# Second product of the self attention with the values stationary, turned back once for four heads

## The reference, cut to what matters

```
x = x + L0_xattn(ctx, ctx, layernorm(x))      # 16 heads of 16
h = layernorm(x)
q, k, v = h @ Wq.T + bq, h @ Wk.T + bk, h @ Wv.T + bv      # 16 heads of 16
scores = q @ k.T / 4                          # 256 x 256 for each head
top_scores, top_idx = top_k(scores, 64)
w = softmax(top_scores)
out = sum_k w[k] * v[top_idx[k]]
x = x + out @ Wo.T + bo
...
```

## Time and profile before

| | |
|---|---|
| median of 3 runs | 1896.39 us (1888.04 to 1904.47) |
| the profiled execution | 1896.86 us, span of its core 1895.4 us |
| TensorE busy | 1518.8 us, 80% of the span |
| VectorE busy | 1291.2 us, 68% |
| ScalarE busy | 984.9 us, 52% |
| GpSimd busy | 402.0 us, 21% |
| granted TensorE clock, mean | 0.896 |

### The profile page before, as it was taken

One profiled execution on the slowest core, in us unless ns is written; L12 is line 12 of the kernel. 1 busy time (PEld: TensorE's weight loads), 2 busy tenths in 40 slices (PEclk: granted clock), 3 DMA queues, 4 the chain that ended last, 5 costly groups with the idle time before them and its releaser, 6 DMA issues. The chain is left out here.

```text
span 1895.4 us, 30782 instructions
## 1 busy us (share of the span) xinstructions
PE 1518.8 (80%) x11554; PEld 910.3 (48%) x11554; DVE 1291.2 (68%) x3823; ACT 984.9 (52%) x1423; POOL 402.0 (21%) x258
## 2 busy tenths in 40 slices
PE   4999999998898988899598979999355666456579
PEld 2555566665555555555355747576212223122243
DVE  3000198887787878778889999512549995699845
ACT  2888777876667757667335434434153331543100
POOL 5000022222221222112211212100104440344200
PEclk9999999999989999989788989999677777687879
DMA  9433333321232213200502221430000000000010
GB/s 165 98 80 68 69 68 68 68 57 35 46 68 57 40 41 68 57 24 2 179 23 67 90 89 45 128 95 1 25 0 0 0 0 0 0 0 0 0 51 17
DMA packets 48209, 94.32 MB, mean 50 GB/s; under 512 B 13345, under 2 KB 36521, under 8 KB 44977
## 3 DMA queue, kind: packets, MB, share of 16 engines
q1 hardware_dynamic: 48048, 92.22, 20.6%
HBM read 91.15 MB, written 1.05 MB: 49 GB/s over the span
## 5 line engine op out<-in xcount | busy, mean ns | idle before, releaser
L982 ACT ACTIVATE attn_arena<-ps 128x1024 f32<-128x1024 f32 x512 | 496.0, 1023 | 224.7 <-PE ps L356 222.8
L356 PE MATMUL ps<-attn_arena 32*128 32x256 f32 x4096 | 377.5, 413 | 6.6 <-ACT attn_arena L982 4.4
L1330 DVE MATCH_REPLACE8 attn_work<-attn_top,attn_work 128x256 f32<-128x256 f32 x896 | 359.4, 408 | 0.0
L1327 DVE MAX8 attn_top<-attn_work 128x8 f32<-128x256 f32 x896 | 332.8, 413 | 0.0
L356 PEld LDWEIGHTS ps<-attn_arena 32*128 32x128 f32 x4096 | 254.7, 190 | 81.9 <-issue 43.3
L368 PE MATMUL ps<-attn_arena 128*32 128x256 f32 x4096 | 286.8, 397 | 5.5 <-issue 5.1
L900 POOL TENSOR_SCALAR attn_pm<-attn_work 128x512 f32<-128x512 f32 x64 | 95.7, 1495 | 643.4 <-DVE attn_work L1330 643.4
L1673 DVE TENSOR_TENSOR_SCAN ssm_h<-ssm_decay,ssm_bu 128x1024 f32<-128x1024 f32 x64 | 219.4, 3467 | 8.2 <-POOL ssm_bu L1466 4.8
L1466 POOL TENSOR_TENSOR ssm_bu<-ssm_brow,ssm_du 128x2048 f32<-128x2048 f32 x32 | 144.6, 4522 | 270.9 <-ACT ssm_brow L1512 230.1
L368 PEld LDWEIGHTS ps<-attn_arena 128*32 128x32 f32 x4096 | 109.9, 111 | 143.8 <-issue 85.1
L1582 PE MATMUL ps<-ssm_hc,ident 128*128 128x512 f32 x256 | 155.1, 763 | 4.5 <-DVE ssm_hc L1678 4.5
(11 more groups left out here) (251 smaller groups left out, 1867.1 us busy)
## 6 DMA issues: line engine op xcount, KB each, us to landing
attn_arena<-ctxT SPq DMA_DIRECT2D x64, 256.0 KB, 8.0
attn_arena<-ctxV SPq DMA_DIRECT2D x16, 1024.0 KB, 13.0
attn_arena<-maskT SPq DMA_DIRECT2D x32, 512.0 KB, 3.7
attn_arena<-ctxT SPq DMA_DIRECT2D x32, 512.0 KB, 4.9
attn_arena<-ctx SPq DMA_DIRECT2D x16, 1024.0 KB, 5.9
ffn_w<-w SPq DMA_DIRECT2D x2, 1024.0 KB, 6.7
X<-x SPq DMA_DIRECT2D x4, 256.0 KB, 3.3
out<-X SPq DMA_DIRECT2D x4, 256.0 KB, 2.2
```

The lines of the kernel that those rows point to most:

```text
L356: mm = pe.matmul(ps[:, first + j - 2 * i, u * S:(u + 1) * S], kx[n % 2][rows, k0:k0 + P], qpad[rows, n % GROUPS, b * S:(b + 1) * S], start ...
L982: act.activation(probs[m % 2][:, 2 * i:2 * i + 2], ps[:, first:first + 2, :], ACT.Exp, scale=1.0 / 16.0).then_inc(exp_done, 1)
L1327: dve.max(top[:, t, turn], s[:, i, t] if turn == 0 else work[:, i, t]).then_inc(picked, 1)
L1330: dve.match_replace(work[:, i, t], top[:, t, turn], s[:, i, t] if turn == 0 else work[:, i, t], LOW).then_inc(picked, 1)
```

## The change

`products` makes the values stationary (32 columns from the head's first, so the next head's columns come along and are not used) and the turned weights move, 256 columns. Head j of a group writes partitions 32j to 32j+31 of `M_`. It is two matmuls a head. `take_sums` copies those 32 partitions, 256 columns, to a new tile `accS`. When the four heads of a group are there, TensorE turns `accS` back with two transposes (`turn_sums`), in slot 0 of step p for the group that ends with head p-2, behind `turn_pm` of head p-1. `divide_self` reads the turned sums from PSUM, and it moves to the end of turn 1's jobs. The semaphore `ao_ready` is gone: `turn_ao` waits for the job's turn in `M_`. The tile v gets 15 more columns and loses its fourth dimension.

```
-        v = sb("v", [P, 2 * T, H, VP])
+        v = sb("v", [P, 2 * T, H * VP + 32 - VP])
+        vh = v[:, :, 0:H * VP].rearrange("p k (h d) -> p k h d", d=VP)
...
-        sums = sb("sums", [P, T, HG, VP])
+        accS = sb("accS", [P, S])
...
+                head = (g * HG + j) * VP
+                for k in range(T):
+                    mm = pe.matmul(M_[32 * j:32 * j + 32, 0:S], v[:, b % 2 * T + k, head:head + 32], pT[:, :, k, :], start=(k == 0), stop=(k == T - 1))
+                mm.then_inc(misc_made, 1)
+
+            def turn_sums(b, g):
+                pe.wait_ge(misc_taken, misc["sums", (b * GROUPS + g + 1) * HG - 1] + 1)
+                begin("self", b, g)
                 for t in range(T):
-                    for k in range(T):
-                        mm = pe.matmul(M_[:, t * VP:(t + 1) * VP], pT[:, t, k, :], v[:, b % 2 * T + k, g * HG + j, :], start=(k == 0), stop=(k == T - 1))
+                    mm = pe.transpose(M_[:, t * P:(t + 1) * P], accS[:, t * P:(t + 1) * P], ident[:])
                 mm.then_inc(misc_made, 1)
 
             def turn_ao(b):
-                pe.wait_ge(ao_ready, GROUPS * (b + 1))
+                pe.wait_ge(misc_taken, misc["self", b, GROUPS - 1] + 1)
...
                         if 0 <= done < B * H:
                             turn_pm(done)
+                        if 0 <= p - 2 < B * H and (p - 2) % HG == HG - 1:
+                            turn_sums(*where(p - 2)[0:2])
...
             def take_sums(p):
-                b, g, j = where(p)
-                if j == 0 and p:
-                    act.wait_ge(ao_ready, GROUPS * b + g)
-                take_misc(sums[:, :, j, :], M_[:, 0:T * VP].rearrange("p (t v) -> p t v", t=T), "sums", p)
+                rows = slice(32 * where(p)[2], 32 * where(p)[2] + 32)
+                take_misc(accS[rows, :], M_[rows, 0:S], "sums", p)
...
             def divide_self(p):
                 b, g, j = where(p)
-                dve.wait_ge(misc_taken, misc["sums", p] + 1)
-                step(dve.reciprocal(srecip[:], sums[:, :, :, D]))
...
+                dve.wait_ge(misc_made, misc["self", b, g] + 1)
+                turned = M_[:, 0:S].rearrange("p (t j v) -> p t j v", t=T, j=HG)
+                step(dve.reciprocal(srecip[:], turned[:, :, :, D]))
...
-                    if 0 <= p - 2 < B * H and (p - 2) % HG == HG - 1:
-                        divide_self(p - 2)
                     for b in due_after("out", p):
...
                     for b in due_after("octx", p):
                         add(b, "octx")
+                    if 0 <= p - 2 < B * H and (p - 2) % HG == HG - 1:
+                        divide_self(p - 2)
```

More of the change, by code:

```diff
@@ L314, in attention @@
         sel_ready, pm_ready, pm_turned, pT_ready = sem("sel_ready"), sem("pm_ready"), sem("pm_turned"), sem("pT_ready")
-        ao_ready = sem("ao_ready")
         moe_loaded, moe_consts, lmax_ready, den_ready = sem("moe_loaded"), sem("moe_consts"), sem("lmax_ready"), sem("den_ready")
@@ L1212, in add_v @@
                 dve.wait_ge(misc_made, misc["v", b] + 1)
-                dve.tensor_tensor(v[:, b % 2 * T:(b % 2 + 1) * T, :, 0:D], M_.rearrange("p (t h d) -> p t h d", t=T, d=D),
+                dve.tensor_tensor(vh[:, b % 2 * T:(b % 2 + 1) * T, :, 0:D], M_.rearrange("p (t h d) -> p t h d", t=T, d=D),
                                   bv[:].rearrange("p (h d) -> p h d", d=D).unsqueeze(1).to_broadcast([P, T, H, D]), ALU.add).then_inc(misc_taken, 1)
@@ L1217, in divide_self @@
                 b, g, j = where(p)
-                dve.wait_ge(misc_taken, misc["sums", p] + 1)
-                step(dve.reciprocal(srecip[:], sums[:, :, :, D]))
-                dve.tensor_tensor(ao[:, :, g * HG * D:(g + 1) * HG * D].rearrange("p t (j d) -> p t j d", d=D), sums[:, :, :, 0:D],
-                                  srecip[:].unsqueeze(3).to_broadcast([P, T, HG, D]), ALU.mult).then_inc(ao_ready, 1)
+                dve.wait_ge(misc_made, misc["self", b, g] + 1)
+                turned = M_[:, 0:S].rearrange("p (t j v) -> p t j v", t=T, j=HG)
+                step(dve.reciprocal(srecip[:], turned[:, :, :, D]))
+                dve.tensor_tensor(ao[:, :, g * HG * D:(g + 1) * HG * D].rearrange("p t (j d) -> p t j d", d=D), turned[:, :, :, 0:D],
+                                  srecip[:].unsqueeze(3).to_broadcast([P, T, HG, D]), ALU.mult).then_inc(misc_taken, 1)
             def choose(b):
```

## The result

The changed kernel takes 1900.08 us (median of 20 runs, 1891.46 to 1904.02), the kernel before 1893.11 us (20 runs, 1882.23 to 1904.47). The ratio is 1.0037, 95% interval 1.0022 to 1.0051: 7 us slower (4 to 10), where 16.4 us were forecast. The profiled execution took 1901.18 us, 1899.6 us from first to last instruction, against 1895.4 before, at a mean granted clock of 0.909 against 0.896.

A forecast was written before the change was run, and what follows sets the result against it. TensorE and ScalarE were taken to set the early pace, VectorE the late one, through GpSimd. Terms: 3.4 (product, turning, copy) + 12.5 (wait) + 0.5 (tail) = +16.4 us on 1896.9, so 1913 us; range 1893 to 1930.

The forecast's parts named there:

- The product on TensorE: Each head's second self attention product: 0.15 us saved by one shape change less, -6.6 us for 44 heads beside L368.
- Turning back: Two new transposes behind turn_pm in slot 0: 0.3 us in each of 11 steps, +3.3 us, plus 0.5 behind head 63.
- The copy: ScalarE's copy of the sums grows from 194 to about 378 ns; the next M_ job waits 37 times: +6.7 us.
- The wait on VectorE: The division at turn 1 waits for transposes behind turn_pm: about 42 us in 15 groups, +12.5 us reaching the end.
- cover in the early steps: In eight steps from 5 to 41, TensorE's waits for ScalarE's exponentials hide VectorE's delay; together 0.5 us remains.
- step 13: A batch's cross attention ends here; the division comes 2.9 us later, only 0.27 is free, so about 2.5 us counts.
- step 61: TensorE waits for GpSimd here, so VectorE's later division counts in full: +1.9 us.
- rival 4: The clock: TensorE idles longer before its pm turns, and two or three more half-clock stretches cost 8 to 11 us; chance 0.10.
- step 46: Follows step 45, where a batch's cross attention ends and the late division was to add about 2.5 us without cover.
- two signs against itself: Wrong if heads 4 to 12's period leaves 54.2 by over 1 us, or L1219 waits yet the last head ends at most 5 us later.

The follow-up runs named there:

- half product: The changed kernel with 128 instead of 256 moving columns in the product and a copy of 34 columns: 1887.38 us, ratio 0.9965 to the kernel before.
- old form with 119 columns: The kernel before, each matmul of its second product moving 119 instead of 17 columns, of which 17 are copied: 1891.68 us, ratio 0.9994.
- short copy: The changed kernel with ScalarE copying 34 instead of 256 columns of each head's 32 partitions: 1894.24 us, ratio 1.0012 to the kernel before.
- short product: The changed kernel with the product moving 17 instead of 256 columns and ScalarE copying those 17: 1874.22 us, ratio 0.9901 to the kernel before.
- the wait alone: The kernel before, with VectorE's division also waiting for the pm transposes of the next step's slot 0: 1907.59 us, ratio 1.0077.
- four heads at once: The changed kernel with turn_sums first and one product and copy per four-head group: 1844.49 us; with the division in turn 3 as well, 1820.13 us.

## Why the prediction was wrong

**The product on TensorE** was right in length: 0.15 us a head forecast, 0.11 + 0.04 read. That all 44 savings lie on the path was not tested in this form, and the half product shows that in some steps a shorter product brings nothing. **Turning back** was right in kind (273 ns a transpose, in slot 0). **The copy** was near: 362 ns for the 378 assumed, 4.7 us measured for 6.7.

**The wait on VectorE** was right in size: 46.3 us of waiting for 42, cover in the early steps, 2.7 for 2.5 us in step 13, 1.9 for 1.9 in step 61; 14 to 15 us for 12.5 when it is added or taken away alone. TensorE's waits for GpSimd grew as said, from 234 to 1208 us; the group of L482 before, and then after:

```profile
L482 PE MATMUL ps<-ident,attn_pm 128*128 128x128 f32 x256 | 44.3, 299 | 42.0 <-POOL attn_pm L903 42.0
```
```profile
L482 PE MATMUL ps<-ident,attn_pm 128*128 128x128 f32 x256 | 45.2, 303 | 53.8 <-POOL attn_pm L912 53.8
```

With the measured wait and copy the terms make -6.6 + 3.3 + 0.5 + 4.7 + 14.6 = +16.5 us, and 7.0 (4 to 10) was measured. Some 9 us are missing; the copy and the wait carry intervals of 5 to 6 us to either side, so this figure is no sharper than that.

**The step that failed is the clock**, which the sum held constant and rival 4 let only fall, because TensorE would stand idle longer in front of its pm turns. It did stand idle longer, and the mean clock rose from 0.898 to 0.907. I had looked at the product's length alone, not at what it moves in that time: before, eight matmuls of 17 columns; after, four of 256, in the same 1 us.

What 0.01 of clock is worth, in us:
- the old form with 119 columns: 3.7 us of work added, -1.1 seen, 4.8 won (0 to 10) for 0.0049: 10
- among the runs of one kernel each, the time falls by 16 to 18 (before, three sets of 23 to 29 runs) and 13 (after, 20 runs); this goes with the clock, and by itself does not say which of the two is the cause
- short copy to half product: 18.8 us of work taken away, 8.9 seen, so at most 9.9 lost for 0.0087: 11
- short copy to short product: 33.1 taken away, 21.0 seen, at most 12.1 lost for 0.0103: 12.

The last two are upper ends, since they count all the work taken away as work on the path. At 10 to 18 us the rise of 0.0091 would bring 9 to 16 us; that much is an estimate.

**A second thing was overlooked: step 46.** The forecast has 2.5 us for heads 44 to 46, without cover, and the trace has -4.0, because TensorE's idle time ahead of L435 fell from 9.54 to 4.51 us. This is not the clock and not one execution's luck. The stretch takes 34.3 to 35.1 us, with 8.9 to 9.5 us ahead of L435, in the four profiles of the old form without the wait, and 28.7 to 31.4 us, with 2.9 to 5.9, in all eight of the new form, those with a mean clock as low as before included. With the wait alone it is 33.5 and 6.5 us. What TensorE waits for there, and why the new form shortens it, stays open.

The clock and step 46 together give back more than is missing, if both are taken at their full size. How the 9 us divide between them is not shown. Two rows speak for a small part of the clock: after head 46 it rose most (0.92 for 0.87 from 917 us on), and the time there is longer by just the 5.7 us forecast; and up to head 44 only 1.6 us of the forecast are missing. The profiled pair also began its head 0 2.5 us apart, which no term explains.

The prediction had named two signs against itself, and neither came: the period of heads 4 to 12 changed by 0.4 us, and the last head does end over 5 us later. Counted from the start of head 0, VectorE starts head 63 6.1 us later than before. So the mechanism of the wait stood; a term for the clock was missing, and the step behind head 45 was read wrongly.

What the row said beforehand: the earlier trace rows was read as a price for more idle time. The same row could have been read from the other side, with some 130 us at half clock in the earlier trace rows as something that a change can also give back.

Shown: with more moved columns the mean clock was higher in either form of the product (0.8973 to 0.9060 in the new one, 0.8983 to 0.9032 in the old one). Not shown: by what. The half product also leaves TensorE 0.43 us a head sooner, to stand idle ahead of its next wait, as in step 10, and these runs don't separate the columns from that; for the old form with 119 the block hardly changed in length, so there the columns are the likelier cause. Nor is it shown why four heads at once, with as many columns moved in all, has only 0.8993.

## What to carry to other kernels

Where a profile has stretches at half clock, the clock is a term of the sum with both signs: ask what a change gives TensorE to do in the same time, not only how long it is busy, and hold the mean clock over many runs beside every ratio. Before a missing amount is put down to the clock, compare the two traces from mark to mark over the whole stretch: here one step held 6.9 us of it, and half clock was in both kernels there. A swap of stationary and moving operand buys nothing by itself; it pays when the column tiles run side by side, so gather the work of a group first (-2.5%, and -3.8% with the division moved). And when a result comes to VectorE by way of TensorE's queue, its place in VectorE's order has to move with it: two turns later were worth 14 us here, 24 us in the grouped version, and nothing in the kernel that did not have the wait.

## What the runs showed of the hardware

- A ScalarE copy of 32 partitions by 256 columns takes 362 ns, one of 128 partitions by 256 columns 378 ns: in these two the partitions hardly count.
- TensorE work that is added can come back by the clock: 119 moved columns in place of 17 made the block 8% longer and the kernel no slower (0.9994), with the mean clock at 0.9032 for 0.8983.
- Two runs of matmuls of the same tile shape follow each other faster: L368 holds TensorE for 1.00 us ahead of a product of another shape and 0.89 ahead of one of its own.
- The clock varies from run to run of one kernel (0.891 to 0.904 before), and the time with it. A single profile of each kernel would not have told 0.898 from 0.907 safely; the means over 12 to 29 runs do.
